# Layer-0 feed-forward with rows gathered per slot eight ahead, and layer-3 attention with work moved between VectorE, ScalarE and GpSimd

## Time and profile before

| | us |
|---|---|
| median of 3 runs | 3355.54 (3344.76 to 3358.28) |
| the profiled execution | 3350.59 |
| its span | 3348.9 |
| layer-0 feed-forward, first run | 13.4 to 271.4 of the span |
| layer-0 feed-forward, second run | 439.3 to 700.7 |
| layer-3 attention | 2653.2 to 3008.3 |
| PE busy | 2403.8 (72%) |
| DVE, ACT, POOL busy | 1590.5, 1083.1, 849.2 |

### The profile page before, as it was taken

The page is one execution under the profiler, slowest core; times in us unless marked ns, Lnnn a source line. Parts: engine busy times, 40 slices in busy tenths (PEclk is TensorE's granted clock), DMA queues, the critical chain, the costliest instruction groups (busy, mean ns, idle before and its releaser), DMA issues. The chain is left out here.

```text
span 3348.9 us, 45143 instructions
## 1 busy us (share of the span) xinstructions
PE 2403.8 (72%) x13128; PEld 1597.5 (48%) x13129; DVE 1590.5 (47%) x3638; ACT 1083.1 (32%) x2400; POOL 849.2 (25%) x759
## 2 busy tenths in 40 slices
PE   2696945953647361098799971495999879889998
PEld 2463533633635360087466650494444435544554
DVE  3466943675257527933333349634111267761110
ACT  1342312422223121064344431263222135563222
POOL 4323433223611361077100010384000112200000
PEclk9997957985578555599899985697999878999999
DMA  7101062033522356066200013265000043310000
GB/s 202 54 20 30 1 171 59 19 97 84 113 56 77 81 109 182 1 132 136 58 1 1 1 38 92 52 144 138 0 0 0 19 100 78 83 43 26 0 0 25
DMA packets 316644, 211.22 MB, mean 63 GB/s; under 512 B 64711, under 2 KB 300171, under 8 KB 313963
## 3 DMA queue, kind: packets, MB, share of 16 engines
q1 hardware_dynamic: 282731, 177.16, 19.5%
q0 software_dynamic: 33792, 32.57, 5.9%
HBM read 147.94 MB, written 61.12 MB: 62 GB/s over the span
## 5 line engine op out<-in xcount | busy, mean ns | idle before, releaser
L159 POOL TENSOR_TENSOR rstd<-ln_t,power 128x4 f32<-128x4 f32 (+1 forms) x96 | 96.9, 1021 | 636.3 <-DVE ln_t L152 635.9
L2286 DVE TENSOR_TENSOR x<-x,s_y 128x512 f32 (+1 forms) x16 | 11.0, 688 | 496.8 <-PE s_y L2365 496.8
L2350 PE MATMUL s_z<-s_ha,s_wt_h 128*128 128x512 f32 x512 | 222.4, 592 | 0.0
L2357 PE MATMUL s_z<-s_hb,s_wt_h 128*128 128x512 f32 x512 | 222.3, 592 | 0.0
L1897 PE MATMUL s_hu<-s_xgt,s_w 128*128 128x128 f32 x768 | 195.3, 399 | 1.7 <-ACT s_xgt L1837 0.9
L2576 DVE TENSOR_REDUCE s_mx<-s_sa 128x2 f32<-128x512 f32 x256 | 167.1, 685 | 61.3 <-PE s_sa L2729 59.9
L2657 ACT ACTIVATE s_e<-s_sc 128x512 f32<-128x512 f32 x256 | 149.6, 599 | 123.9 <-PE s_sc L2745 122.4
L1897 PEld LDWEIGHTS s_hu<-s_xgt,s_w 128*128 128x128 f32 x768 | 186.7, 327 | 3.0 <-issue 3.0
L188 PE MATMUL s_tp<-ident,xn 128*128 128x128 f32 x352 | 71.5, 339 | 152.1 <-DVE xn L178 148.1
L1883 PE MATMUL s_lp<-ident,s_posf 48*128 48x48 f32 x2 | 0.6, 312 | 233.6 <-DVE s_prob L1765 233.6
L1706 POOL DMA_INDIRECT s_xg<-rows_dram,s_from_i x96 | 95.8, 998 | 269.2 <-DVE s_to_i L1769 240.5
(11 more groups left out here) (406 smaller groups left out, 5687.6 us busy)
## 6 DMA issues: line engine op xcount, KB each, us to landing
s_w<-in_L_ffn_W_dram SPq DMA_DIRECT2D x96, 256.0 KB
s_kx<-k_dram SPq DMA_DIRECT2D x16, 576.0 KB
s_qx<-q_dram SPq DMA_DIRECT2D x48, 192.0 KB
s_w<-in_L_ffn_w_dram SPq DMA_DIRECT2D x2, 4096.0 KB, 14.4
s_b<-in_L_ffn_b_dram SPq DMA_DIRECT2D x16, 512.0 KB, 7.1
acc_dram<-s_zero SPq DMA_DIRECT2D x16, 512.0 KB, 6.2
acc_dram<-x SPq DMA_DIRECT2D x4, 2048.0 KB, 9.7
x<-acc_dram SPq DMA_DIRECT2D x16, 512.0 KB, 7.0
```

Source lines behind the costliest of these rows:

```text
L159: pool.tensor_tensor(core.rstd[:, tiles], core.ln_t[:, 2, tiles], core.power[:, 0:CT], ALU.pow).then_inc(s.scale_ready.sem, 1)
L2350: last = pe.matmul(z[:, o, :], wt["h1"][:, f, o * P:(o + 1) * P], ha[:, f, :], start=f == 0, stop=f == HB - 1)
L2357: last = pe.matmul(z[:, o, :], wt["h2"][:, f, o * P:(o + 1) * P], hb[:, f, :], start=f == 0, stop=f == HB - 1)
```

## The change

**Data.** x, its statistics, `rstd` and a new `nmr` (minus mean times rstd) become columns of one tensor `fields` [128, 32, 136]. All stages use x through it.

**Layer-0 feed-forward.** Weights and constants are held in SBUF over the first three stages (`L0Weights`), and loaded only in the first run. POOL no longer copies rows. After the places are known nothing is scattered: the list of tokens of each slot is computed by one-hot matrices on DVE and 32 small matmuls on PE. x with its fields was stored in order to DRAM (`x_dram`); POOL gathers the 128 rows of each slot directly from it, eight slots ahead, and scatters the result to `y_dram`. ACT normalises the gathered rows as it copies them. There are 39 slots. b2 goes in by one more bfloat16 matmul per slot (L705). DVE adds y to the gathered x in the slot and makes its statistics there; the tail only loads `fields` back. The routing loops are unrolled.

**Layer-3 attention.** Normalisation (`normal`) and the copy of v (`keep_v`) go from DVE to ACT, the split of the maxima and the residual addition from DVE to POOL (ACT copies y out of PSUM first, `keep_y`), statistics are made later on DVE. Stores and loads of parts are counted per batch; the first q split is on POOL.

```diff
-        self.x = sb("x", [P, TILES, D])
+        self.fields = sb("fields", [P, TILES, D + 8])
+        self.x = self.fields[:, :, 0:D]
+        self.sums = self.fields[:, :, D:D + 6]
+        self.rstd = self.fields[:, :, D + 6]
+        self.nmr = self.fields[:, :, D + 7]
...
+        self.SLOTS = TILES + self.EXPERTS - 1
...
+            sp.wait_ge(nmr_ready.sem, nmr_ready.past(0))
+            sp.dma_start(x_dram[1:TOKENS + 1, :].rearrange("(p t) d -> p t d", p=P), core.fields[:, :, :]).then_inc(x_stored.sem, 16)
...
+                sp.dma_start(core.fields[:, q * 8:(q + 1) * 8, :],
+                             y_dram[1:TOKENS + 1, :].rearrange("(p t) d -> p t d", p=P)[:, q * 8:(q + 1) * 8, :]).then_inc(loaded_back.sem, 16)
...
-            for t in range(TILES):
-                pool.indirect_dma_start(sorted_dram, bass.IndirectOffsetOnAxis(ap=pos_i[:, t:t + 1], axis=0),
-                                        sent[:, t, :], None).then_inc(scattered.sem, 16)
...
+            def gather(i):
+                if i >= 2:
+                    pool.wait_ge(gathered[i % 2].sem, 16 * (i // 2))
+                pool.indirect_dma_start(xg[:, i, :], None, x_dram,
+                                        bass.IndirectOffsetOnAxis(ap=ids[:, i:i + 1], axis=0)).then_inc(gathered[i % 2].sem, 16)
...
+            for i in range(LEAD):
+                gather(i)
+            pool.wait_ge(to_ready.sem, 1)
             for i in range(SLOTS):
+                if i + LEAD < SLOTS:
+                    gather(i + LEAD)
                 pool.wait_ge(y_kept.sem, y_kept.past(i))
...
+                pool.indirect_dma_start(y_dram, bass.IndirectOffsetOnAxis(ap=to_ids[:, i:i + 1], axis=0),
+                                        xg[:, i, :], None).then_inc(stored.sem, 16)
...
+            dve.tensor_tensor(slot_hot[:, :, :], parts[:, 0, :].unsqueeze(2).to_broadcast([P, TILES, SLOTS]),
+                              held.count[:, 0:SLOTS].unsqueeze(1).to_broadcast([P, TILES, SLOTS]),
+                              ALU.is_equal).then_inc(slots_hot.sem, 1)
...
+            for t in range(TILES):
+                last = dve.tensor_scalar(lane[:, t, :], held.count[:, :], parts[:, 1, t:t + 1], None, ALU.is_equal)
...
+                dve.tensor_tensor(xi, yp[:, 0:P].unsqueeze(1), xi, ALU.add).then_inc(y_taken.sem, 1)
...
+                dve.drain()
+                dve.bn_stats(xg[:, bass.ds(i, 1), D:D + 6], xg[:, bass.ds(i, 1), 0:D]).then_inc(y_kept.sem, 1)
...
+                act.activation(xs[:, u, :], xg[:, one, 0:D], ACT.Identity,
+                               bias=xg[:, one, D + 7:D + 8], scale=xg[:, one, D + 6:D + 7]).then_inc(xs_ready.sem, 1)
...
+            for t in range(TILES):
+                if t % CT == 0:
+                    pe.wait_ge(lane_ready.sem, lane_ready.past(t // CT))
+                last = pe.matmul(ha[:, 1, 0:2 * SLOTS], lane[:, t, :], slot_id[:, t, :, :].rearrange("p a n -> p (a n)"),
+                                 start=t == 0, stop=t == TILES - 1)
...
+                pe.matmul(yp[:, 0:P], held.ones_b[:, :], b2[:, bass.ds(e, 1), :], start=True, stop=False)
...
+            def body(c, u, before, after):
+                for i in range(2):
+                    b = 2 * c + i
+                    if i == 0 or after:
+                        split_maxima(b + 1, 1 - i)
+                    if i == 0 and after > 1:
+                        split(c + 2, 0, 2 * c + 1)
+                    if i or before:
+                        add(b - 1)
+                    if i == 0 and after > 1:
+                        split(c + 2, 1, 2 * c + 2)
...
+            def normal(c, u):
+                act.wait_ge(nmr_ready.sem, nmr_ready.past(c))
+                act.wait_ge(s.tp_ready.sem, s.tp_ready.past(c - 2))
+                for j in range(CT):
+                    t = bass.ds(c * CT + j, 1)
+                    last = act.activation(core.xn[:, u, j, :], core.x[:, t, :], ACT.Identity, bias=nmr[:, t], scale=core.rstd[:, t])
+                last.then_inc(s.xn_ready.sem, 1)
```

More of the change, by code:

```diff
@@ L328, in _ @@
[L328 to L334, removed]
@@ new lines, in _ @@
+            ln_scales_pool(pool, core, s, range(2, CHUNKS))
+            pool.wait_ge(x_stored.sem, 32 if load else 16)
+            pool.wait_ge(ids_ready.sem, 1)
+            def gather(i):
[5 more added lines that the diff above has]
+                gather(i)
@@ L386, in _ @@
+            for u in range(2):
+                pool.wait_ge(gathered[u].sem, 16 * ((SLOTS + 1 - u) // 2))
             pool.wait_ge(stored.sem, 16 * SLOTS)
-            pool.wait_ge(scattered.sem, 16 * TILES)
             s.reset_pool_dmas(pool)
@@ L422, in _ @@
             dve.drain()
-            dve.tensor_tensor(hot[:, :, :], hot[:, :, :], by_expert(rev, TILES, True), ALU.mult)
+            dve.tensor_tensor(hot[:, :, :], hot[:, :, :], by_expert(held.rev, TILES, True), ALU.mult)
             dve.drain()
@@ L552, in _ @@
             ln_pe(pe, core, s, 0, 0)
-            pe.wait_ge(router_loaded.sem, 32)
-            def route(c, u, more=True):
-                if more:
-                    ln_pe(pe, core, s, c + 1, 1 - u)
+            if load:
+                pe.wait_ge(router_loaded.sem, 32)
+            for c in range(CHUNKS):
+                if c + 1 < CHUNKS:
+                    ln_pe(pe, core, s, c + 1, 1 - c % 2)
                 pe.wait_ge(s.xnt_ready.sem, s.xnt_ready.past(c))
@@ L2550, in _ @@
-            each_pair(pool, 2, CHUNKS, split)
+                pool.wait_ge(pj_kept.sem, pj_kept.past(2 * c + n))
+                for i in range(2):
+                    pool.wait_ge(parts_stored[n][i].sem, stored_by(c, n))
+                pool.tensor_tensor(parts[:, n, 0, :], proj[:, n, :], nothing, ALU.add).then_inc(split_step.sem, 1)
+                pool.wait_ge(split_step.sem, split_step.past(3 * at))
+                pool.tensor_tensor(left[:, n, :], proj[:, n, :], parts[:, n, 0, :], ALU.subtract).then_inc(split_step.sem, 1)
@@ new lines, in add @@
+            def add(b):
+                xs = rows(core.x, b * NT, NT)
+                pool.wait_ge(y_kept.sem, y_kept.past(b))
+                pool.tensor_tensor(xs, xs, yk[:, :, :], ALU.add).then_inc(x_added.sem, 1)
+            split(0, 1, 0)
+            ln_scales_pool(pool, core, s, range(2, CHUNKS))
+            pool.wait_ge(m3_clear.sem, 1)
+            split_maxima(0, 0)
+            def body(c, u, before, after):
+                for i in range(2):
+                    b = 2 * c + i
[7 more added lines that the diff above has]
+                        split(c + 2, 1, 2 * c + 2)
@@ L2935, in build @@
         begin(core)
+        with stage(nc) as kept:
+            held = L0Weights(core, kept)
+            l0_ffn(core, held, True)
+            l0_attn(core)
+            l0_ffn(core, held, False)
         for run in STAGES:
```

530 lines of the change are left out of this document (312 added, 218 removed).

## The result

The changed kernel takes 3239.51 us (median of 4 runs), the kernel before 3352.93 in the same comparison: a ratio of 0.9655, 95% interval 0.9623 to 0.9687. The forecast was 3230. One of the four executions was disturbed (8146.85 us): the ratio leaves it out, the median of four counts it, and the median of the other three is 3238.32. The profiled execution took 3238.32, its span is 3236.6, so 112.3 us less than before. The total is near the forecast's -121.8, but not for the reasons given: layer 0 gave more than its -99.0, and layer-3 attention, which was to give 22.8, became longer.

The account below looks back on a forecast made before the run. Layer-0's first part was taken as a latency chain, its slots as PE-bound, layer-3 attention as waiting for DVE's maxima. Layer 0 -99.0 and layer 3 -22.8 took 3350.6 to 3228.8, stated as 3230 us, range 3197 to 3268.

Parts of the forecast that it names:

- Step 1: Layer-0 feed-forwards, places known to first slot: 14.3 us replaces 52.4 and 55.5, saving 38.1 and 41.2.
- Step 2: Layer-0 routing: PE's wait during POOL's padding fill goes, 3.7 us saved per feed-forward; weight loads stay hidden.
- rival B: Layer-0 slots or loads become longer, 3260 us; weights held back by the x store add 20 once; chance 0.13.
- Step 3: Layer-0 slots: one fewer, -3.35 us per feed-forward; b2 matmul 0.10 a slot, +3.9 per feed-forward; other work hidden.
- Rival C: Layer-0 slots: POOL and DVE hold each other up, about 3410 us, slower than before; chance 0.03.
- Has eight slots of lead: Layer-0 slots: the gather, issued eight slots ahead, was taken as hidden, at no cost.
- Step 4: Layer-0 feed-forwards, last scatter to next stage: 12.7 us instead of 19.4, -6.7 in each.
- Step 5: Layer-3 attention: PE's waits for DVE's maxima and the slow clock go, -26.5 and -2.5 us; POOL's chain charged 3.
- rival A: Layer-3 attention: PE's wait for the maxima comes back on POOL, about 3269 us; chance 0.08.
- my three signs of being wrong: Slot pitch over 3.7 us, list over 20 us, or PE waiting for POOL's maxima over 1 us a batch.
- no stretch at clock 0.5 after the first batches: Layer-3 attention, expected in the new profile: PE's granted clock not at 0.5 past the first batches, batches 17 to 18 us.
- Step 6: Layer-3 attention, normalisation on ACT: +0.74 us in six chunks, 4.4 in all; -2.3 at the start, +1.1 at the end.

Follow-up runs that it names:

- run 10: Changed kernel with the bfloat16 b2 product made twice in each layer-0 slot: 3236.46 us (ratio 0.9617).
- runs 11, 12: Changed kernel with rows gathered four, then five, slots ahead instead of eight: 3477.73 us, then 3264.36 us.
- Run 3: Changed kernel with SyncE placing the next chunk's maxima before issuing later loads in layer-3 attention: 3207.21 us (0.9551).
- run 6: Changed kernel with the maxima's split back on VectorE and POOL's split of q ahead of the residual addition: 3253.39 us (0.9684).
- run 4: Changed kernel with ScalarE's own queue issuing the maxima's placement, SyncE's order of loads kept: 3257.11 us (0.9696).
- run 7: Changed kernel with placement ahead of the loads and six chunks' rows normalised on VectorE again: 3202.14 us (0.9525).

## Why the prediction was right, and where it was not

- **Step 1, places to first slot**: right, -80.5 for -79.3. The one-hot row was 5.29 / 32 = 0.165 us for my 0.20. By the page's four elements a cycle in place of two (the Trainium skill, VectorE: DVE Perf Modes, the perf-mode tier table), half the fp32 row's 0.28 us would make some 4.4 us for the 32, an estimate; the measured 5.29 lies between it and my 6.4.
- **Step 2, routing**: -9.8 for -7.4. The weights were not late: from ACT's first copy to PE's first product g it is 3.19 us in the first run (63.21 to 66.40) and 3.18 in the second, where no weights are loaded. The mishap of the late x store in rival B did not come.
- **Step 3, slots**: this term was mis-sized, +7.8 for b2, where it is 0 (run 10). 39 instead of 40 slots gave -8.1 over both, for -6.7 + 7.8. Rival C's place can be read: DVE's instructions in the slots keep 0.68 to 0.69 us and POOL's transfers 0.97 to 0.99, so neither holds the other up in the trace. The rule of "DVE blocks DMA" (the Trainium skill, SBUF — State Buffer, under "SBUF: two separate sides") would have shown as late gathers, and none was late here. The rule is for two-port instructions, and no row tells whether one of these is, so this does not test it. "Has eight slots of lead" was enough and wrong as a reason: four of them are not to be had (runs 11, 12).
- **Step 4, tail**: -16.5 for -13.4.
- **Step 5, the step that failed.** The maxima went as forecast: POOL's five instructions start 0.32 us apart, 1.5 in all for my 2.2, and PE does not wait for them in steady batches, so rival A fell. The failed sentence is "Behind POOL's chain stand the splits of k and q; they end some 5 us later, and their loads are needed a chunk later". They ended later and were not needed sooner, but the placement, which PE needs 3 us after its issue, is issued 4 us behind them and lands late. Run 3 shows it by the order alone and run 6 by earlier loads; run 4 shows that it is not SyncE's queue. It took back the whole -26.5 and more: +12.3 for -22.8. None of my three signs of being wrong would have caught it: they ask for a long slot, a long list or a wait for POOL's maxima. What caught it was "no stretch at clock 0.5 after the first batches", which did not hold.
- **Step 6, normalisation on ACT**: charged 0.74 a chunk, measured 2.0 (run 7). At full clock it is 0.75 to 1.0, so the charge was about right; most of the rest, 7.5 us, lies in two halves with a slower clock, a cost for which step 6 had no term.
- With the order mended layer-3 attention is 26.5 us below the kernel before, at 327.8 (run 3), where the forecast had 331.5. That this agrees is in part luck. Step 5 took the half of 17.0 us to have neither wait nor slow clock, and these windows of the kernel before show its first 2 us at 0.51:

```profile
2847.42:2849.40 1.98, 1.98 (x13) 1.52 (x10) 0.85 (x2) 0.46 (x1) 0.00 (x0) 0.51 0.04 8
2849.40:2852.00 2.60, 2.60 (x29) 1.18 (x27) 2.41 (x6) 1.91 (x4) 0.00 (x0) 1.00 0.59 163
```

  At full clock a chunk takes 15.2 + 18.6 = 33.8 us in run 3, where step 5 had 17.0 + 18.0 and steps 5 and 6 charged 1.1 more. Against that stand run 3's two halves with a slower clock.

The total came near by luck. Layer 3 missed by 35.1 us. Layer 0's terms were all a little cautious and gave 15.9 more than forecast, and 9.7 came from stages that the forecast had at 0; together they offset 25.6 of it.

## What to carry to other kernels

When work moves ahead of an engine's next steps, ask not only when its results are needed but which transfers it pushes later, and what small, urgent transfer these then meet. A small transfer is best issued ahead of the large loads, not beside them in another queue. The lead of a prefetch has to be counted from the instruction that the prefetch stands behind in its own queue, less the slots that the other engines' program orders keep in flight.

## What the runs showed of the hardware

- A placement of 3 x 8 KB lands 1.9 us after issue where 1152 KB of loads were issued 9.8 us before it or earlier (run 6), 2.9 where it was 8.6 (changed kernel), and 4.6 to 5.4 where it was 4.0 to 4.1. Through ScalarE's queue it takes 4.6 to 5.4 as well, and 8.0 once: another queue gave it no way past the loads.
- Three DMA issues of ScalarE take 1.8 to 2.6 us, and in the rows shown its next activation waits 2.30.
- A 128x128 bfloat16 product between fp32 products of PE took 0.05 us of a slot that PE fills, though its own row reads 0.22, and under 0.02 us a slot over the stage, where the next slot hid it (run 10).
- A wait of PE can cost more than its length: 17 us of waits taken away gave 39 between the first profile and run 3. Behind the wait of 4.03 us the granted clock was 0.50, the level of 1.2 GHz, from 2740 to 2748 us of the changed kernel (window below), and back at 0.99 after that. Not every wait did it: one of 1.72 us was followed by 1.00 (run 7), and 23.47 us for a half without a wait, at 0.64, came behind a half with a wait of 3.16.

```profile
2740.00:2744.00 4.00, 3.97 (x21) 1.90 (x22) 2.03 (x4) 2.67 (x6) 0.00 (x0) 0.50 0.77 133
```
